# A perceiver in one kernel: cross attention with its gates drawn apart, self attention with a longer lag, a feed-forward's loads moved into its norm

## The reference

```python
Pn = rmsnorm(P, input_norm_w)
k_proj, v_proj = Pn @ Wk.T, Pn @ Wv.T
for _ in range(3):
    q_proj = rmsnorm(slots, slot_norm_w) @ Wq.T
    attn = softmax(einsum('bkd,bmd->bkm', q_proj, k_proj) * SCALE, axis=-2)
    attn = attn / (sum(attn, axis=-1) + EPS)
    updates = einsum('bkm,bmd->bkd', attn, v_proj)
    r = sigmoid(xr + hr); z = sigmoid(xz + hz); n = tanh(xn + r * hn)
    slots = (1.0 - z) * n + z * slots
```

## Time and profile before

| | us |
|---|---|
| median of three runs | 3792.14 (3792.0 to 3793.28) |
| profiled execution | 3802.4 |
| its span | 3800.6 |
| PE busy | 3413.3 (90%) |
| DVE busy | 2029.4 (53%) |
| ACT busy | 1694.6 (45%) |
| POOL busy | 681.8 (18%) |
| layer 1's cross attention loop, first scores to the last turn's | 1358.9 to 1850.7 |
| layer 1's self attention loop | 1914.8 to 1968.1 |
| layer 3's self attention loop | 3706.1 to 3767.6 |

### The profile page before, as it was taken

The page is one execution under the profiler, slowest core; times in us unless marked ns, Lnnn a source line. Parts: engine busy times, 40 slices in busy tenths (PEclk is TensorE's granted clock), DMA queues, the critical chain, the costliest instruction groups (busy, mean ns, idle before and its releaser), DMA issues. The chain is left out here.

```text
span 3800.6 us, 90636 instructions
## 1 busy us (share of the span) xinstructions
PE 3413.3 (90%) x39440; PEld 2399.6 (63%) x39440; DVE 2029.4 (53%) x4136; ACT 1694.6 (45%) x3093; POOL 681.8 (18%) x334
## 2 busy tenths in 40 slices
PE   6999999879998979999869997999999689998975
PEld 4677767657775667878644354777777555554553
DVE  4666666654443267776654364556565442333336
ACT  3776777523331177777525352444444331111222
POOL 0777677310110000000021011010100000000001
PEclk9999999889998989999978998999999889999986
DMA  1111111030101415334010001111110013220710
GB/s 62 54 37 37 37 54 37 2 98 28 36 1 58 152 46 186 131 114 155 16 50 1 0 0 48 58 40 57 43 54 21 24 33 106 92 77 3 255 35 16
DMA packets 155254, 223.54 MB, mean 59 GB/s; under 512 B 39375, under 2 KB 134539, under 8 KB 154732
## 3 DMA queue, kind: packets, MB, share of 16 engines
q1 hardware_dynamic: 154860, 217.75, 17.3%
HBM read 216.67 MB, written 1.05 MB: 57 GB/s over the span
## 5 line engine op out<-in xcount | busy, mean ns | idle before, releaser
L3172 POOL TENSOR_TENSOR x_sc<-x_sc,h_T 128x2048 f32<-128x2048 f32 (+1 forms) x105 | 442.5, 4252 | 227.6 <-ACT h_T L3383 227.6
L2988 ACT ACTIVATE x_sc<-x_sc,x_nb 128x2048 f32<-128x2048 f32 (+1 forms) x112 | 210.6, 1880 | 297.4 <-DVE x_sc L3037 297.3
L3037 DVE SCALAR_TENSOR_TENSOR x_sc<-ps,x_nb,x_cap 128x2048 f32<-128x2048 f32 (+1 forms) x112 | 246.2, 2198 | 49.1 <-PE ps L2929 49.1
L3457 DVE TENSOR_TENSOR x_most<-x_most,ps 128x512 f32<-128x512 f32 (+1 forms) x352 | 234.6, 685 | 59.5 <-PE ps L3289 33.8
L1735 ACT ACTIVATE s1i_both<-ps,s_less,s_rs_s 128x64 f32<-128x64 f32 x624 | 214.0, 425 | 41.7 <-DVE s_less L1846 41.7
L3362 ACT COPY x_sc<-ps 128x1024 f32<-128x1024 f32 x192 | 179.2, 943 | 90.7 <-PE ps L3289 53.0
L3376 ACT ACTIVATE x_sc<-x_sc 128x2048 f32<-128x2048 f32 (+1 forms) x112 | 200.6, 1792 | 25.2 <-POOL x_sc L3172 21.1
L3245 PE MATMUL ps<-x_wv,x_ctx_T 128*128 128x256 f32 (+1 forms) x832 | 204.5, 388 | 0.0
L2900 PE MATMUL ps<-x_ctx_T,x_wk 128*128 128x401 f32 (+1 forms) x512 | 200.0, 517 | 1.5 <-PEq L44 1.5
L3237 PE MATMUL ps<-x_ctx_T,x_wk 128*128 128x401 f32 (+1 forms) x512 | 197.5, 524 | 3.4 <-POOL x_v L3201 3.4
L2908 PE MATMUL ps<-x_wv,x_ctx_T 128*128 128x256 f32 (+1 forms) x832 | 197.7, 379 | 0.0
(11 more groups left out here) (518 smaller groups left out, 6809.6 us busy)
## 6 DMA issues: line engine op xcount, KB each, us to landing
x_ctx_T<-in_ctx_T SPq DMA_DIRECT2D x32, 1601.0 KB
s1i_ctx_T<-in_ctx_T SPq DMA_DIRECT2D x16, 1601.0 KB, 7.5
x3i_ctx_T<-in_ctx_T SPq DMA_DIRECT2D x16, 1601.0 KB, 6.7
s1i_ctx_n<-in_ctx SPq DMA_DIRECT2D x16, 1536.0 KB
x3i_ctx_n<-in_ctx SPq DMA_DIRECT2D x16, 768.0 KB
h<-in_ctx SPq DMA_DIRECT2D x12, 896.0 KB
e_w<-in_L_attn_W SPq DMA_DIRECT2D x8, 1024.0 KB, 7.3
rows<-in_ctx SPq DMA_DIRECT2D x12, 640.0 KB
```

Of the source, the lines that this page charges most:

```text
L2988: nc.scalar.activation(x, x, ACT.Square, scale=DH ** -0.5, bias=nb[0:keys, 0:1]).then_inc(squared, 1)
L3037: nc.vector.scalar_tensor_tensor(out=slot[0:keys].rearrange("p r m h j q -> p (r m h) (j q)")[:, :, 0:width], in0=score_banks[0:keys].rear ...
L3172: return eng.tensor_tensor(x, x, most_of, ALU.subtract)
L3457: ins = nc.vector.tensor_tensor(best[0:keys, rs], best[0:keys, rs], score_banks[0:keys, rs, :, j, :], ALU.max)
```

## The change

In the cross attention EARLY goes from 12 to 9; ACT's gates are split, the reset gate placed ahead of the last unit's exponentials; DVE's update is split, the candidate placed ahead of the last weighing; and DVE's squares of loaded halves go ahead of finish_prepare and finish_norms. In the self attention the turn lags by three steps instead of two, weigh by four instead of three, the projection by six instead of five, and the ring has five buffers. In the feed-forward the block of loads goes; the first list is issued by SP inside the norm's block, the later list by SP in the stage itself behind two memsets, and all five memsets are done by POOL at the stage's start, with waits for them on PE and DVE. The diff, cut to its core:

```diff
-    EARLY = 12
+    EARLY = 9
...
-                        def exponentials(h):
+                        def exponentials(h, units):
                             lane = h % LANES
-                            for u, (b, c, tiles) in enumerate(UNITS):
+                            for u in units:
+                                b, c, tiles = UNITS[u]
...
-                        def gates(h):
+                        def reset_gate(h):
                             act.wait_ge(r_done, h + 1)
                             for m in range(KT):
                                 nc.scalar.activation(rz[:, m, :], ps[:, 6, m * P:(m + 1) * P],
                                                      ACT.Tanh, scale=0.5, bias=gb2[:, m:m + 1]
                                                      ).then_inc(gates_r, 1)
+
+                        def other_gates(h):
                             act.wait_ge(n_in, h + 1)
...
-                            exponentials(h)
+                            exponentials(h, range(NU - 1))
                             if h:
-                                gates(h - 1)
+                                reset_gate(h - 1)
+                            exponentials(h, [NU - 1])
+                            if h:
+                                other_gates(h - 1)
...
-                        gates(TURNS - 1)
+                        reset_gate(TURNS - 1)
+                        other_gates(TURNS - 1)
...
-                        def update(h):
+                        def candidate(h):
                             dve.wait_ge(n_done, h + 1)
...
                                 ALU.add).then_inc(n_in, 1)
+
+                        def update(h):
                             dve.wait_ge(n_out, KT * (h + 1))
...
                             weigh(h, 2)
+                            if h:
+                                candidate(h - 1)
                             weigh(h, 3)
                             if h:
                                 update(h - 1)
...
+                            for j in half_jobs(h):
+                                square(j)
                             if h + 1 < TURNS:
                                 finish_prepare(h + 1)
                                 finish_norms(h + 1)
-                            for j in half_jobs(h):
-                                square(j)
                         finish_sum(TURNS - 1)
                         take_turned(TURNS - 1)
+                        candidate(TURNS - 1)
                         update(TURNS - 1)
...
-    RING = 4
+    RING = 5
...
-    WEIGHS, OUT = 3, 5
+    TURN, WEIGHS, OUT = 3, 4, 6
...
-                    if 0 <= n - 2 < T:
-                        turn(n - 2)
+                    if 0 <= n - TURN < T:
+                        turn(n - TURN)
...
-                    if 0 <= n - 2 < T:
+                    if 0 <= n - TURN < T:
+                        t = n - TURN
                         for m in range(KT):
-                            act.wait_ge(turned, KT * (n - 2) + m + 1)
-                            if m == 0 and n - 2 >= 2:
-                                act.wait_ge(u_done, n - 3)
+                            act.wait_ge(turned, KT * t + m + 1)
+                            if m == 0 and t >= 2:
+                                act.wait_ge(u_done, t - 1)
...
-            with nc.Block() as block:
-
-                @block.vector
-                def _(dve):
-                    nc.vector.memset(eb2[:, :], 0.0).then_inc(pads, 1)
...
-                @block.sync
-                def _(sp):
-                    for dst, src in first:
-                        sp.dma_start(dst, src).then_inc(first_in, 16)
-                    sp.wait_ge(pads, 2)
-                    for dst, src in later:
-                        sp.dma_start(dst, src).then_inc(later_in, 16)
-
-            layernorm(nc, env, "g1_ln", env.x, env.h, env.h_T)
+            layernorm(nc, env, "g1_ln", env.x, env.h, env.h_T, begun=first, begun_in=first_in)
...
+                    @block.sync
+                    def _(sp):
+                        sp.wait_ge(pads, 2)
+                        for dst, src in later:
+                            sp.dma_start(dst, src).then_inc(later_in, 16)
+
                     @block.gpsimd
                     def _(pool):
+                        nc.gpsimd.memset(eb2[:, :], 0.0).then_inc(pads, 1)
+                        pool.wait_ge(pads, 1)
+                        nc.gpsimd.memset(sw2[HD:P, :], 0.0).then_inc(pads, 1)
+                        pool.wait_ge(pads, 2)
+                        nc.gpsimd.memset(blocks[:, :, :, :], 0.0).then_inc(pads, 1)
+                        pool.wait_ge(pads, 3)
+                        nc.gpsimd.memset(sh_T[HD:P, :], 0.0).then_inc(pads, 1)
+                        pool.wait_ge(pads, 4)
+                        nc.gpsimd.memset(sh_T[HD:HD + 1, :], 1.0).then_inc(pads, 1)
+                        pool.wait_ge(pads, 5)
                         nc.gpsimd.tensor_copy(cur[:, :, :], env.h[:, :, :]).then_inc(state, 1)
...
                                 if n == 0 and s_ == 0:
                                     pe.wait_ge(later_in, 16 * len(later))
+                                    pe.wait_ge(pads, 5)
...
                         dve.wait_ge(first_in, 16 * len(first))
+                        dve.wait_ge(pads, 3)
```

More of the change, by code:

```diff
@@ L2110, in _ @@
                         nc.scalar.activation(x, x, ACT.Exp, scale=scale).then_inc(exped, 1)
-                    if 0 <= n - 2 < T:
+                    if 0 <= n - TURN < T:
+                        t = n - TURN
                         for m in range(KT):
-                            act.wait_ge(turned, KT * (n - 2) + m + 1)
-                            if m == 0 and n - 2 >= 2:
-                                act.wait_ge(u_done, n - 3)
+                            act.wait_ge(turned, KT * t + m + 1)
+                            if m == 0 and t >= 2:
+                                act.wait_ge(u_done, t - 1)
                             nc.scalar.copy(
-                                p_T[n % 2][:, m, :, :, :].rearrange("p r j q -> p (r j q)"),
+                                p_T[t % 2][:, m, :, :, :].rearrange("p r j q -> p (r j q)"),
                                 ps[:, 4 + m, :]).then_inc(p_out, 1)
@@ L2363, in l1_ffn @@
         with signals(nc, "g1_in", "first_in later_in pads") as (first_in, later_in, pads):
-            with nc.Block() as block:
-                @block.vector
-                def _(dve):
-                    nc.vector.memset(eb2[:, :], 0.0).then_inc(pads, 1)
-                    nc.vector.memset(sw2[HD:P, :], 0.0).then_inc(pads, 1)
-                    nc.vector.memset(blocks[:, :, :, :], 0.0).then_inc(pads, 1)
-                    nc.vector.memset(sh_T[HD:P, :], 0.0).then_inc(pads, 1)
-                    dve.wait_ge(pads, 4)
-                    nc.vector.memset(sh_T[HD:HD + 1, :], 1.0).then_inc(pads, 1)
-                @block.sync
-                def _(sp):
-                    for dst, src in first:
-                        sp.dma_start(dst, src).then_inc(first_in, 16)
-                    sp.wait_ge(pads, 2)
-                    for dst, src in later:
-                        sp.dma_start(dst, src).then_inc(later_in, 16)
-            layernorm(nc, env, "g1_ln", env.x, env.h, env.h_T)
+            layernorm(nc, env, "g1_ln", env.x, env.h, env.h_T, begun=first, begun_in=first_in)
             with signals(nc, "g1", "own filled act_taken dve_taken shifted exped neg picked state "
```

## The result

The changed kernel takes 3754.8 us (median of four runs, 3750.5 to 3761.2), the kernel before 3792.7 on the same occasions: a ratio of 0.9900, 95% interval 0.9883 to 0.9917. The forecast was 3751.8 with a range of 3743 to 3765. The profiled execution took 3754.86 us, span 3753.1; the one before 3802.4, so the two traces differ by 47.5 us, more than the medians (37.9): the trace before is some 10 us above its kernel's median.

A forecast was written before the change was run, and what follows sets the result against it. PE was taken to bound cross attention's turns, the order of work the other touched loops. Gains of 16.6 + 3.8 + 6.0 + 12.9 + 1.0 = 40.3 us off the median 3792.1 gave 3751.8, range 3743 to 3765.

The forecast's parts named there:

- Part 1: Cross attention: earlier gates, candidate and sum of squares shorten 22 turns to 19.85 us; minus 16.6 us, bounds 7 and 22.
- the 0.7 lost between turns 0 and 1: Cross attention: DVE gets 2.9 us of squares into a pause of some 2.2; 0.7 us lost.
- The 1.6 of the first turn: Cross attention: 1.6 us assumed for the first turn's low clock, which stays and is not gained.
- The seven times 0.25 for two halves: Cross attention: squaring two loaded halves ahead of the reciprocal delays the query, 0.25 us in each of 7 turns.
- the slower rival: Cross attention: late-landing loaded squares ahead of reciprocal and query delay the next scores; 3793 us and up, chance 0.02.
- PE free at S+19.85: Cross attention: PE ends a turn's work 19.85 us after its scores start, with the query done at S+18.8.
- Part 2, first call: First self attention: turning a step later removes PE's wait for POOL; five steps take 24.0 instead of 26.7; minus 3.8 us.
- Second call: Second self attention, with bias: five steps take 28.9 us instead of 33.5, and 1.4 gained in the tail; minus 6.0.
- Part 3: Feed-forward: loads issued inside the norm start it earlier, PE waiting for the last landing; minus 12.9 us, bounds 11 and 14.3.
- Clock, minus 1: Feed-forward's start: without the loads' block PE may start at 2.4 GHz; minus 1 us, bounds 0 and 2.
- Query last: Rival, cross attention: DVE's reciprocal still ends a turn, leaving 0.42 us in 22 turns, 9.3 us; 3761, chance 0.15.
- Low clock in self attention: Rival: turns starting a step later keep the clock low longer, losing the 9.8 us gain; 3761.6, chance 0.15.

The follow-up runs named there:

- Part 2 alone: The kernel before with only the self attention's extra step between scores and turn, in both calls; ratio 0.9980.
- the whole: The changed kernel with all its edits, run once more on the same chip as its parts, against the kernel before; ratio 0.9905.
- the last kernel: Changed kernel plus early add, ACT's copies first, four loads behind, loaded squares behind the reciprocal, 12 matmuls ahead of norms' transposes; 3743.2 us, ratio 0.9853.

## Why the prediction was right

The total was right, the median being 3.0 us over the forecast. That it is so close is in part luck: the touched stages give 43.7 us in the traces, 3.4 more than the sum, and the medians 37.9, 2.4 less. By its steps:

- **Part 1, minus 16.6: 20.0 in the trace (17.5 to 18.4 in the four others with this code and these norms).** The offsets held within 0.4 us, the 0.7 lost between turns 0 and 1 included. Two terms were mis-sized, in opposite ways. The turn is 19.62, not 19.85: I took PE's own work as the turn before less its idle 0.42. But the last tile stands there with 0.65 us, where no scores follow at once (turn 8 of the kernel before, in the row below); in the changed kernel four tiles take 1.78 from 1541.30 to 1543.08, 0.45 each. 22 x 0.23 = 5.1 us more gained. And what stays above the plain turns is 442.6 - 22 x 19.62 = 11.0 us, where I had 6.0 + 1.6 + 1.8 = 9.4. The 1.6 of the first turn, for which no row had stood, is what it took: 21.22 less 19.62, with the clock low until 1384.8. The seven times 0.25 for two halves did not come, and it would have been five times, since five of these 22 turns have two halves; instead the late landings, which I had only as the slower rival, made two of those turns wait for the query, 1.8 us in all. The mechanism of that rival is real, and its size here is a twentieth of what it needed.

```profile
1556.38 0.65 PE L1668 MATMUL ps<-s1i_ctx_n,s1i_both 128*64 128x257 f32 x4
```

- **I gave the gain to the chain as a whole, and that holds:** of 20.0 us, early gates and candidate bring 7.0 without the nine tiles, the nine tiles 1.5 without them (the loaded squares moved in both), and 11.5 come only with both. The step "PE free at S+19.85" hid that PE, and not the query, ends the turn.
- **Part 2, first call, minus 3.8: 2.6 between the two traces, 4.6 with Part 2 alone.** Steps of 4.59 at low clock, with scores of 2 us, as I had them (4.6), then 5.12 before the first projection and 5.15 and 5.13 with it (5.1). Third to eighth step: 24.6 us, forecast 24.0; 23.0 to 24.8 over all profiles of this code, by the clock (see the rivals).
- **Second call, minus 6.0: 6.6.** Right in sum, wrong in its parts. The five steps took 26.9 us, not 28.9: at clock 0.50 the steps without a projection took DVE's 5.0, and not the 7 that I had given PE. The tail gained nothing (18.85 us from the last bias add to the last add, 18.79 before) where I had 1.4: it goes through the add, which I had counted as 0.4 us of DVE's time and not as a link in a loop.
- **Part 3, minus 12.9: 13.2** (14.35 less 1.2 of landing; I had 1.4). The landing varies: the first product came 9.5 to 10.8 us behind the norm's start in seven kernels, forecast 10.2. The ratios show less of it, as said: 7.6 us alone (4 to 11), and some 7 to 25 by the whole with and without it. Why is open. POOL's memsets took 0.73 to 0.96 us each, 4.3 in all (4.0 forecast), and were hidden.
- **Clock, minus 1: not there.** The first eight products took 5.53, 3.62, 6.54 and 5.20 us in the four kernels with the loads' block, and 4.98 to 6.51 in seven without it. A block in which PE did nothing was not what set the clock, or not alone: the norm itself leaves PE idle for 4.55 us ahead of its transposes.
- **The rivals.** Query last: no; of the waits for the query in 23 turns three are left. Low clock in self attention: real, and small. The first call's clock was 0.76 instead of 0.78 and its low stretch some 3 us longer. In the whole's second trace, with the same code, the clock rose within the fifth step: its scores took 1.12 us, DVE waited 0.29 for them, and fifth and sixth step took 4.18 and 4.79 us instead of 5.12 and 5.15. So the longer low stretch costs 1.3 us, not 9.8; the steps of 4.59 stood in the sum with their low clock. In the second call the clock rose to 0.75. The Trainium skill's rule ("TensorE: Matmul & The Clock Gate", section "HAM oscillation — how this bites in real kernels"), that pauses between bursts throw PE back to the low clock, agrees with the traces: 0.50 again in the second call, at the feed-forward's start, and in cross attention behind the pause of 2.73 us. What it would cost is decided by who bounds the step.

## What to carry to other kernels

Where a turn ends at the later of several near-equal chains, cost every pair of edits and not only each: in cross attention two edits bring 7.0 and 1.5 us one without the other and 20.0 together, in self attention nothing each and about 2.5 together. A wait that vanishes from a list while the stage keeps its length has moved to the next link; look for the link that the list calls "issue". And a consumer of a late transfer should not stand ahead of the chain that ends the loop, even where it usually has the time: here it cost 1.8 us of waits and 0.7 in turn 0.

## What I had not expected of the hardware

The same instructions take two lengths from execution to execution, by where the clock falls. The interval from the kernel's first norm to its second took 753.7 to 756.5 us in eight of the profiles and 748.8 to 751.1 in the six others, whichever edits they had. The clock in 50 to 100 us is the visible difference: 0.88 to 0.89 in the eight, 0.93 to 0.94 in the six. For the kernel before:

```profile
50.00:100.00 50.00, 41.60 (x453) 29.80 (x449) 33.28 (x55) 27.48 (x33) 8.88 (x2) 0.88 0.08 28
```

and for the changed one:

```profile
50.00:100.00 50.00, 43.02 (x453) 30.48 (x453) 32.66 (x54) 28.41 (x33) 10.66 (x5) 0.93 0.10 34
```

The feed-forward varied from 340.8 to 348.3 us over all profiles. Gains of a few microseconds can't be read from two spans, only from the intervals of the stages concerned.

Twelve or 24 matmuls into a bank that nobody reads brought the transposes of the norms from 421 to 273 ns each (median of 160 instructions).

In cross attention PE stands still for 0.1 to 2.7 us inside the scores or the gate products of a few turns, before and after, and the trace names nothing that it waits for ("issue", 4.1 us in the list above and 1.2 at the gate products). Turns 5 and 11 have such a pause in thirteen of the fourteen profiles, turn 17, 7, 9 or 13 in some; in the last kernel it stands in turns 6 and 12. In turns 5, 11 and 17, when the next pairs' columns and rows are loaded, the DMA engines were busy for 0.94 to 0.99 of the time in the traces of the two kernels, but a pause of 1.0 us stands in turn 7 at 0.25. What PE waits for was not tried.
